# Flamingo decoder block on one core: rotation tables and low projection weights prepared on GpSimd, MLP and expert weights prepared in smaller pieces

## What is computed

```python
x = x + tanh(g_xattn[0]) * cross_attention_L0(x, ctx)          # 16 heads of 8
for l in range(2):                                             # the gated inner model, DEPTH = 2
    qkv = shift_token(y) @ wqkv[l]                             # 128 x 1536, 8 heads of 64
    q, k = rotary_xpos(l2norm(q) * q_scale[l], l2norm(k) * k_scale[l])
    y = y + local_attention(q, k, v) @ wo[l]                   # windows of 64
    h = layernorm(shift_token(y)) @ w1[l] + b1[l]              # 128 x 682
    y = y + (h_a * gelu(h_g)) @ w2[l] + b2[l]
x = x + tanh(g_ffn[0]) * y
x = x + tanh(g_xattn[1]) * cross_attention_L1(x, ctx)
x = x + tanh(g_ffn[1]) * experts(layernorm(x))                 # 8 experts, 128 x 1536 in all, top 2
```

## Time and profile before

| | |
|---|---|
| median of 3 runs | 1170.15 us (1168.88 to 1170.16) |
| the profiled execution | 1167.68 us |
| its span, first to last instruction | 1165.9 us |
| mean granted TensorE clock | 0.977 of full speed |
| PE busy | 1072.5 us, 92% |
| DVE busy | 969.5 us, 83% |
| ACT busy | 931.3 us, 80% |
| POOL (GpSimd) busy | 752.3 us, 65% |

### The profile page before, as it was taken

How to read it: one execution, slowest core, us unless ns; L and a number is a source line. 1 busy time by engine, 2 the same in 40 slices (tenths; PEclk the granted TensorE clock), 3 DMA queues, 4 the chain that set the end, 5 groups by cost and what they waited for, 6 DMA issues and landing times.

```text
span 1165.9 us, 33073 instructions
## 1 busy us (share of the span) xinstructions
PE 1072.5 (92%) x11244; PEld 910.6 (78%) x11244; DVE 969.5 (83%) x2215; ACT 931.3 (80%) x2588; POOL 752.3 (65%) x1164
## 2 busy tenths in 40 slices
PE   6899976999999979979999999989889997999996
PEld 3777754888887869967888878788867776799996
DVE  4799968988988866778889888757889997599988
ACT  4898966999998977759999989966678886877672
POOL 4799936777767766637777676636779994344431
PEclk9999989999999999999999999989989999999999
DMA  7000000211111101101112311100000000000000
GB/s 208 17 2 1 2 14 18 56 29 29 24 30 31 25 18 28 25 15 29 28 26 46 83 27 24 25 15 15 5 1 2 2 2 1 6 15 12 15 14 17
DMA packets 53158, 28.67 MB, mean 25 GB/s; under 512 B 36949, under 2 KB 47233, under 8 KB 52994
## 3 DMA queue, kind: packets, MB, share of 16 engines
q1 hardware_dynamic: 50370, 25.83, 9.0%
q10 hardware_dynamic: 2624, 0.72, 0.3%
HBM read 9.77 MB, written 2.10 MB: 10 GB/s over the span
## 4 chain that ended last, share of the span: by engine, by line
PE 61%; DVE 13%; ACT 11%; issue 8%; POOL 6%; DMA 0%; ACTq 0%; DVEq 0%; POOLq 0%
PE m_ps_y L1602 7%; PE a_ps_b L1057 5%; PE a_ps_t L1068 5%; PE a_ps_s L963 4%; PE a_ps_a L990 4%; PE a_ps_t L1032 4%; PE a_ps_qk L947 4%; DVE x_e L708 3%; PE f_ps_y L1370 2%; PE a_ps_qk L948 2%; PE a_ps_qk L949 2%; ACT a_e L1135 2%; PE a_ps_s L1004 2%; PE m_ps_h L1589 2%; ACT x_e L669 2%
## 5 line engine op out<-in xcount | busy, mean ns | idle before, releaser
L1135 ACT ACTIVATE a_e<-a_ps_s,a_stat 128x128 f32<-128x128 f32 x512 | 227.0, 481 | 5.0 <-DVE a_stat L1204 5.0
L1266 POOL TENSOR_TENSOR a_rot<-a_rot 128x512 f32<-128x512 f32 x64 | 82.8, 1293 | 135.6 <-DVE a_rot L1158 135.6
L1260 POOL TENSOR_TENSOR a_e<-a_e,a_stat 128x1024 f32<-128x1024 f32 x64 | 121.5, 1899 | 2.6 <-DVE a_stat L1183 2.6
L1135 ACT ACTIVATION_READ_ACCUMULATOR a_e<-a_ps_s,a_stat 128x1 f32 x512 | 117.2, 229 | 0.0
L1254 POOL TENSOR_TENSOR a_rot<-a_rot 128x512 f32<-128x512 f32 x64 | 81.7, 1276 | 19.6 <-DVE a_rot L1158 19.6
L757 DVE TENSOR_REDUCE x_stat<-x_ps_s 128x16 f32<-128x1024 f32 x64 | 77.1, 1205 | 11.9 <-PE x_ps_s L563 11.9
L1156 DVE TENSOR_TENSOR a_rot<-a_ps_qk,a_rtab 128x512 f32<-128x512 f32 x128 | 86.9, 679 | 0.0
L1158 DVE TENSOR_TENSOR a_rot<-a_ps_qk,a_rtab 128x512 f32<-128x512 f32 x128 | 86.9, 679 | 0.0
L1200 DVE TENSOR_REDUCE a_stat<-a_ps_s 128x8 f32<-128x1024 f32 x64 | 77.8, 1216 | 4.6 <-PE a_ps_s L963 4.5
L1068 PE MATMUL a_ps_t<-c,a_e 128*128 128x128 f32 x512 | 71.7, 284 | 9.9 <-POOL a_e L1260 6.7
L1193 DVE TENSOR_REDUCE a_stat<-a_sq 128x16 f32<-128x1024 f32 x64 | 77.9, 1218 | 3.1 <-ACT a_sq L1142 1.5
(11 more groups left out here) (222 smaller groups left out, 3685.0 us busy)
## 6 DMA issues: line engine op xcount, KB each, us to landing
a_vx<-a_vt SPq DMA_DIRECT2D x64, 128.0 KB, 2.3
a_h<-y SPq DMA_DIRECT2D x64, 32.0 KB
out_dram<-x SPq DMA_DIRECT2D x32, 64.0 KB, 1.5
a_h<-y SPq DMA_DIRECT2D x64, 31.8 KB
f_h<-y SPq DMA_DIRECT2D x32, 63.5 KB
wqkv<-in_L_ffn_wqkv_dram SPq DMA_DIRECT2D x2, 768.0 KB, 4.8
w<-in_L_ffn_w_dram SPq DMA_DIRECT2D x2, 768.0 KB, 5.5
x<-in_x_dram SPq DMA_DIRECT2D x1, 768.0 KB, 5.3
```

What stands on the lines that cost most here:

```text
L1135: act.activation(self.e[n % 2][:, P * i:P * i + P], ps_s[:, P * i:P * i + P], ACT.Exp, bias=stat[:, 24 + i:25 + i], scale=stat[:, root:roo ...
L1260: p.tensor_tensor(e3, e3, self.stat[n % UNROLL][:, 16:24].unsqueeze(2).broadcast_to([P, 8, P]), ALU.mult)\
L1266: p.tensor_tensor(r, r, self.rot2[:, INNER:], ALU.add).then_inc(self.s_n, 1)
```

## The change

The two VectorE preparations of local attention move to GpSimd: the tables in a new function `tables` at s = -3, and `wqr` in three pieces of 128x512 at s = -2, -1 and 0. VectorE waits for the tables at s = 1. The MLP's preparation begins two steps earlier (PREP = -8) and is spread over four: ScalarE's two roundings at s = -8 and -7, the pads at s = -7, GpSimd's two subtractions at s = -6 and -5. The experts' subtractions become eight of 128x192, at MLP 1's odd steps 13 to 27; ScalarE's four roundings stay.

```diff
-PREP = -6
+PREP = -8
@@ Local.vector
         if s == -3:
             if not l:
                 settle(v, self.setup.totals())
-            v.wait_ge(g.s_aw, g.n_aw * (l + 1))
-            for u in range(UPS):
-                for i, src in enumerate((g.cos_t, g.sin_t)):
-                    w = 2 * LD
-                    v.tensor_tensor(self.rtab[:, nt * i + w * u:nt * i + w * u + w], src[:, w * u:w * u + w],
-                                    g.scl[:, w * i:w * i + w], ALU.mult).then_inc(self.s_tab, 1)
+        if s == 1:
             v.wait_ge(self.s_tab, 4 * (l + 1))
-        if s == -2:
-            v.wait_ge(self.s_wh, l + 1)
-            v.tensor_tensor(self.wqr[:, :], g.wqkv[:, :], self.wqh[:, :], ALU.subtract).then_inc(self.s_wr, 1)
@@ Local.tensor, s == 0
-            pe.wait_ge(self.s_wr, l + 1)
+            pe.wait_ge(self.s_wr, 3 * l + 3)
@@ Local, new
+    def tables(self, p, l):
+
+        g, nt, w = self.g, UPS * 2 * LD, 2 * LD
+        p.wait_ge(g.s_aw, g.n_aw * (l + 1))
+        for u in range(UPS):
+            for i, src in enumerate((g.cos_t, g.sin_t)):
+                p.tensor_tensor(self.rtab[:, nt * i + w * u:nt * i + w * u + w], src[:, w * u:w * u + w],
+                                g.scl[:, w * i:w * i + w], ALU.mult).then_inc(self.s_tab, 1)
@@ Local.gpsimd
+        if s == -3:
+            self.tables(p, l)
+        if -2 <= s < 1:
+            part = slice(INNER * (s + 2), INNER * (s + 2) + INNER)
+            p.wait_ge(self.s_wh, l + 1)
+            p.tensor_tensor(self.wqr[:, part], g.wqkv[:, part], self.wqh[:, part], ALU.subtract).then_inc(self.s_wr, 1)
@@ Mlp.scalar
-        if s == PREP:
+        if PREP <= s < PREP + 2:
...
-            act.activation(self.w1h[:, 0:HID], g.mw1[:, HID:2 * HID], ACT.Copy).then_inc(self.s_wh, 1)
-            act.activation(self.w1h[:, 3 * P:3 * P + HID], g.mw1[:, 0:HID], ACT.Copy).then_inc(self.s_wh, 1)
+            at, lo = ((0, HID), (3 * P, 0))[s - PREP]
+            act.activation(self.w1h[:, at:at + HID], g.mw1[:, lo:lo + HID], ACT.Copy).then_inc(self.s_wh, 1)
@@ Mlp.gpsimd
-        if s == PREP:
-            if not l:
-                self.pads(p)
+        if s == PREP + 1 and not l:
+            self.pads(p)
+        i = s - PREP - 2
+        if 0 <= i < 2:
...
-        if l and s in (13, 17, 21, 25):
-            self.experts.low(p, s // 4 - 3)
+        if l and 13 <= s < 29 and s % 2:
+            self.experts.low(p, (s - 13) // 2)
@@ Experts.low
-        at = slice(CH * P // 4 * i, CH * P // 4 * i + CH * P // 4)
-        p.wait_ge(self.s_wh, i + 1)
+        at = slice(CH * P // 8 * i, CH * P // 8 * i + CH * P // 8)
+        p.wait_ge(self.s_wh, i // 2 + 1)
```

More of the change, by code:

```diff
@@ L935, in sync @@
             sp.wait_ge(self.s_wh, 1)
-            sp.wait_ge(self.s_wr, 1)
+            sp.wait_ge(self.s_wr, 3)
             load_attention_weights(sp, self.g, 1, 0)
@@ L1164, in vector @@
         ps_qk, ps_t, ps_a, ps_b, ps_s = self.banks[l]
-        nt = UPS * 2 * LD
         if s == -3:
@@ L1481, in gpsimd @@
     def gpsimd(self, p, l, s):
-        if s == PREP:
-            if not l:
-                self.pads(p)
+        if s == PREP + 1 and not l:
+            self.pads(p)
+        i = s - PREP - 2
+        if 0 <= i < 2:
             after(p, self.s_a, 3 * T // 2 * l)
[L1486 to L1489, removed]
+            at, lo = ((0, HID), (3 * P, 0))[i]
+            p.wait_ge(self.s_wh, 2 * l + i + 1)
+            p.tensor_tensor(self.w1l[:, at:at + HID], self.g.mw1[:, lo:lo + HID], self.w1h[:, at:at + HID], ALU.subtract)\
+                .then_inc(self.s_wl, 1)
         n = s - 1
@@ L1582, in tensor @@
                     pe.wait_ge(self.s_wh, 4)
-                    pe.wait_ge(self.s_wl, 4)
+                    pe.wait_ge(self.s_wl, 8)
                     self.take(pe, l, "h")
```

## The result

| | before | changed |
|---|---|---|
| median of 20 runs, on one chip | 1170.8 us | 1164.7 us |
| ratio, with its 95% interval | | 0.9944 (0.9933 to 0.9955) |
| the profiled execution | 1167.68 us | 1164.99 us |
| its span | 1165.9 us | 1162.5 us |
| mean granted TensorE clock | 0.977 | 0.975 |

The account below looks back on a forecast made before the run. TensorE, busy for 92% of the span, was taken as the bound, so its few gaps were priced. -3.0 + 0.9 - 0.5 - 2.8 - 1.4 = -6.8 us, from a median of 1170.15 to 1163.4 us, range 1159.0 to 1168.0.

Parts of the forecast that it names:

- The likeliest case: Whole kernel: the forecast itself, all terms summing to -6.8 us, 1163.4 us; chance 0.45.
- Local attention 0: Where it is taken in: VectorE's preparation leaves the waits of L562 and most of a low-clock stretch goes; -3.0 us.
- Local attention 1: Where it is taken in: GpSimd's moved work becomes a wait ahead of L1043; +0.9 us.
- The preparations: MLP 0 and MLP 1: gaps go, but late pieces cost about 0.6 us each; -0.5 and -2.8 us.
- The tie: Softmax in the MLP preparations: VectorE's 8-column product is held until GpSimd's instruction ends, 0.77 instead of 0.20 us.
- The sign: MLP preparations: five steps of about 8.2 us instead of 7.6, with a product of about 1 us in each.
- Rival A: MLP preparations: no tie, later GpSimd ends are absorbed; -6.4 us there, 1160.3 us in all; chance 0.20.
- The low clock in MLP 1: MLP 1's preparation: slow matmuls behind the 2.47 us gap, 1.5 us beyond it, were to go with the gap.
- Experts' pieces: MLP 1: halved pieces shorten the chain by 0.36 us, four times, new pieces between hidden; -1.4 us.
- Rival B: Local attention: taking in gives little, -1.0 us, the second wait is 1.2, experts give nothing; 1167.0 us; chance 0.24.
- C: MLP preparations: each of five late pieces brings a low-clock stretch; slower, +4.4 us, 1174.6 us; chance 0.03.
- D: Whole kernel: small effects cancel, no difference, 1168 to 1171 us; chance 0.08.

Follow-up runs that it names:

- e1: The kernel before with only the local-attention moves (rotation tables and three wqr pieces on GpSimd): 0.9986 of before (0.9966 to 1.0006).
- e2: The kernel before with only the MLP's preparations in pieces over four steps: 0.9949 of before (0.9925 to 0.9974).
- e3: The kernel before with only the experts' low parts in eight pieces instead of four: 0.9986 of before (0.9970 to 1.0002).
- e4: The changed kernel with VectorE's two-input 128x8 product replaced by a one-input reduction, query-norm factor left out (measurement only): 0.9863 of before (0.9837 to 0.9889).
- e5: The changed kernel with the MLP's pads and GpSimd pieces issued behind the softmax multiply, in GpSimd's idle gap: 0.9886 of before (0.9860 to 0.9912).
- e10: The kernel before with only the second local attention's rotation tables and wqr moved to GpSimd: 1.0031 of before (1.0016 to 1.0047).
- e8: As e5, but the second local attention's tables and wqr on VectorE as before: 0.9907 of before (0.9875 to 0.9939).
- e12: As e8, with the MLP's layer-norm roots of its first four steps also in GpSimd's gap: 0.9900 of before (0.9876 to 0.9924).

## Why the prediction was right

The forecast was 1163.4, the time 1164.7; against the time of before beside it, -6.8 was forecast and -6.6 measured by the ratio. The likeliest case came true by its steps. That the totals agree within 0.2 us is luck in part: three sizes were off, all three in the same direction, so that the places sum to -8.2, and 1.6 us that no term has stand against them.

- **Local attention 0, -3.0.** Measured -3.4 by the shift, in the changed kernel, in its second profile, and in e1. In e2 and e3, which don't have the move, the same place gained 0.6, because the low-clock stretch fell 5 us earlier (granted clock 0.72 from 154 to 160 us, where before has 1.00); so 2.8 to 3.4 is the move's. Up to the second L562 the shift grew by 2.1, as forecast. The other 1.3 (forecast 0.9) came where the clock had been low. There the prediction was right only up to the landmark: it expected most of the stretch to go with the gap, and the stretch fell behind the first L1043 instead, 0.66 from 166 to 171 us.
- **Local attention 1, +0.9.** +0.6. The mechanism is as described (GpSimd's last piece, then L1043 with nothing between). The term was over-sized: the seven instructions took 5.2 us, not 5.3 (four tables in a row 1.52 instead of 1.68, three pieces 3.75 instead of 3.66), and the last root came 2.9 us earlier than before where TensorE, at its last L1338, was 2.7 us earlier.
- **The preparations, -0.5 and -2.8.** -0.51 and -2.68. The tie is shown by e4 and e5. The price of "say 0.6" a piece measured 0.61 (1.84 for three) and 0.65 (1.30 for two); a piece alone takes 0.92 us, not 0.87. The sign was to be five steps of about 8.2 us; the same excess is spread over seven, three near 8.3 and four of 7.84 to 7.98, and the product took 0.99 to 1.22 us in each of the five, as forecast. Rival A would have been -6.4, which is what e5_gap gets by removing the cause.
- **The low clock in MLP 1.** The prediction let it go with the 2.47 us gap. The stretch at 693 us is in all four kernels that have the pair ahead of the softmax multiply (before, e1, e3, e10; granted clock 0.93 from 676 to 700 us), and in none of the other ten profiles (1.00 in the same window); the gap of 2.41 at MLP 0 has none in any of them. So it went with the gap, but the gap's length alone doesn't make it.
- **Experts' pieces, -1.4.** -2.2: mis-sized. I took the piece's own shortening as 0.36 us, four times, from a slope of 1.9 ns a column and a piece of 0.96; the earlier trace rows have 1.00, and the half piece takes 0.59 to 0.60, so it is 0.41. The roots behind the piece became 0.14 us shorter as well, which the prediction put at nothing; that makes the 0.54 each. Why these roots are slower behind the larger piece was not tested. The new pieces between added nothing, as I had taken it.
- **Sum.** The places sum to -8.2 in both profiles and the times to -6.6 and -5.7. The 1.6 to 2.5 us between them lie outside the edited places. One such place shows in the profiles: from the first L1043 to 213 us the changed kernel gives back 1.6 us in its first profile (granted clock 0.79 from 182 to 190 us), nothing in its second (1.00), and e5_gap gives back 3.3 (0.52). The prediction has no term for it. How much of the timed difference it makes on average, the single profiles can't say. e10's time, 3 us over its wait, would more than cover it, but e8 and e12 don't confirm it. That part is open.
- **GpSimd against VectorE.** The 1.96 that the prediction takes from the Trainium skill, "GPSIMD Engine Reference", section "Performance versus the Vector engine", was measured there for an addition and not for a product. Here `wqr`, a subtraction, took 3.75 us on GpSimd and 1.74 on VectorE, 2.16 times as long.
- **Rival B** fell with L562's second wait, **C** with the transposes' 1.06 to 1.09 us in every long step, **D** with the interval.

## What to carry to other kernels

When work is moved to GpSimd, ask not only whether its queue has room but which VectorE instruction with two SBUF inputs will now meet a longer GpSimd one: an 8-column product of 0.2 us became 1.2 us, and everything queued behind it paid. Put the work behind the instruction that has the deadline, into the gap that is already there; the same pieces cost 3.1 us ahead of the softmax multiply and nothing that the steps show behind it. And for effects of a few microseconds compare the same instruction in two traces over one place: that repeated within 0.02 us, where the ends of two profiles of one kernel lay 6 us apart.

## What the runs showed of the hardware that I had not expected

- Two executions of the same program have their low-clock stretches at different places, and their spans differ by 6.4 us (1162.5 and 1156.1) at a mean granted clock of 0.975 and 0.984. One profile's total is therefore no measure of a change of this size.
- The hold also happens with no edit near it. Where the first local attention runs out, the product takes 1.63 us in the changed kernel, because 1.1 us of layer-norm roots have made the softmax multiply late. A small tie of this kind is paid for in several places of a kernel before anyone looks for it.
- GpSimd's prices: a 128x512 subtraction 1.28 us alone and 1.25 in a row, 128x341 0.92, 128x192 0.59, and four 128x128 products in a row 1.52.
